# Gated delta-rule attention and feed-forward block: the recurrence written out step by step with fewer transfers, and the rounded feed-forward weights kept on chip

## What is computed

```
q, k, v = silu(conv4(x Wq^T)), silu(conv4(x Wk^T)), silu(conv4(x Wv^T))
beta    = sigmoid(x Wb^T)
# delta rule, chunks of 32 tokens per head, with q and k l2-normed, kb = beta k, vb = beta v
T = inverse(I + strict_lower(kb k^T)) ;  u = T vb ;  w = T kb
step(S): u_adj = u_i - w_i S ;  o_i = q_i S + causal(q_i k_i^T) u_adj ;  S = S + k_i^T u_adj
local_s, local_m, local_l = causal filters of 3, 15 and 63 taps per channel over v
p = softmax((x gate_w + gate_b) / exp(log_temp)), mixed with eps
o = p0 local_s + p1 local_m + p2 local_l + p3 delta + p4 v
x = layernorm(x + rmsnorm(o, norm_w) Wo^T)
h = silu(x W1^T s1) * (x W2^T s2) ;  h = gelu(h H1^T s) ;  h = gelu(h H2^T s)
out = layernorm(x + h W3^T s3)
```

## Time and profile before

| | us |
|---|---|
| median of 3 runs | 2368.65 (2364.51 to 2372.69) |
| the profiled execution, its own time | 2375.07 |
| its span in the profile | 2373.2 |
| project, about 0 to 343 | 343 |
| weights_fir, to about 577 | 234 |
| delta, to about 1036 | 459 |
| ffn, to the end | 1337 |
| TensorE busy (share of the span) | 2094.9 (88%) |
| VectorE / ScalarE / GpSimd busy | 1159.3 / 864.9 / 529.7 |
| bytes moved by DMA | 237.59 MB in 244242 packets |

### The profile page before, as it was taken

How to read it: one execution, slowest core, us unless ns; L and a number is a source line. 1 busy time by engine, 2 the same in 40 slices (tenths; PEclk the granted TensorE clock), 3 DMA queues, 4 the chain that set the end, 5 groups by cost and what they waited for, 6 DMA issues and landing times.

```text
span 2373.2 us, 43639 instructions
## 1 busy us (share of the span) xinstructions
PE 2094.9 (88%) x16936; PEld 1776.2 (75%) x16936; DVE 1159.3 (49%) x1825; ACT 864.9 (36%) x1406; POOL 529.7 (22%) x563
## 2 busy tenths in 40 slices
PE   7888873775888878759999999999999999999998
PEld 5776763675777767648888888888888888888886
DVE  5777768953467657642432343233234324432332
ACT  4545542010333323223443444344334434443442
POOL 1113787864445444410000000000000000000000
PEclk9999996797899988869999999999999999999999
DMA  3775667876778777750000000000000000000000
GB/s 123 199 199 171 200 191 182 284 255 207 201 216 221 210 214 205 209 216 34 19 0 18 18 15 3 18 18 0 18 18 18 0 18 18 10 8 18 18 1 18
DMA packets 244242, 237.59 MB, mean 100 GB/s; under 512 B 145938, under 2 KB 203794, under 8 KB 238354
## 3 DMA queue, kind: packets, MB, share of 16 engines
q1 hardware_dynamic: 227218, 193.74, 28.0%
q10 hardware_dynamic: 16896, 41.95, 5.7%
HBM read 139.96 MB, written 95.68 MB: 99 GB/s over the span
## 4 chain that ended last, share of the span: by engine, by line
PE 53%; issue 1%; DVE 1%; ACT 1%; DMA 0%; POOL 0%; DVEq 0%; SPq 0%; ACTq 0%; POOLq 0%
PE B L1636 48%; PE O L1664 5%; PE T L1592 1%; DVE yb L1763 0%; ACT gate L1702 0%; DMA x<-x_s 0%; DVE stats L1794 0%; ACT L1702 0%; DVE z L1789 0%; DVE xl L1743 0%; DVE z L1785 0%; DVE z L1808 0%; ACT xh L1690 0%; POOL rstd L1844 0%; DVEq L1758 0%
## 5 line engine op out<-in xcount | busy, mean ns | idle before, releaser
L1636 PE MATMUL B<-act1l,wr 128*128 128x512 f32 x1024 | 398.4, 389 | 0.0
L1636 PE MATMUL B<-act0h,wr 128*128 128x512 f32 x1024 | 398.3, 389 | 0.0
L1636 PE MATMUL B<-act0l,wr 128*128 128x512 f32 x1024 | 398.3, 389 | 0.0
L1636 PE MATMUL B<-act1h,wr 128*128 128x512 f32 x1024 | 398.3, 389 | 0.0
L1716 ACT ACTIVATE yb<-B,scol 128x512 f32<-128x512 f32 x256 | 176.2, 688 | 581.0 <-PE B L1636 581.0
L1751 DVE TENSOR_TENSOR act0l<-yb,act0h 128x512 fp32r<-128x512 f32 x256 | 176.1, 688 | 377.8 <-ACT act0h L1719 375.7
L1841 POOL TENSOR_TENSOR rstd<-mv,ln_eps 128x4 f32<-128x4 f32 x16 | 3.2, 199 | 1308.2 <-DVE mv L1802 1308.2
L449 DVE SCALAR_TENSOR_TENSOR acc<-proj,taps,acc 128x512 f32<-128x512 f32 x288 | 214.3, 750 | 86.4 <-ACT acc L395 77.9
L1751 DVE TENSOR_TENSOR act1l<-yb,act1h 128x512 fp32r<-128x512 f32 x128 | 88.6, 692 | 295.5 <-ACT act1h L1719 295.5
L1636 PEld LDWEIGHTS B<-act0h,wr 128*128 128x128 f32 x1024 | 192.2, 188 | 39.9
L1636 PEld LDWEIGHTS B<-act1h,wr 128*128 128x128 f32 x1024 | 192.2, 188 | 39.9
(11 more groups left out here) (171 smaller groups left out, 3234.5 us busy)
## 6 DMA issues: line engine op xcount, KB each, us to landing
qk_s<-yT SPq DMA_DIRECT2D x16, 1024.0 KB, 6.3
kk_s<-kfull SPq DMA_DIRECT2D x16, 1024.0 KB, 6.3
qk<-qk_s SPq DMA_DIRECT2D x32, 512.0 KB, 5.3
wraw<-in_ffn_w ACTq DMA_DIRECT2D x32, 352.0 KB, 6.1
wr_s<-wround ACTq DMA_DIRECT2D x32, 352.0 KB, 4.0
toe<-in_toe_short ACTq DMA_DIRECT2D x32, 320.0 KB, 7.4
xt<-in_xt SPq DMA_DIRECT2D x16, 524.0 KB, 4.3
k_s<-ktok SPq DMA_DIRECT2D x16, 512.0 KB, 7.1
```

Source lines behind the costliest of these rows:

```text
L1636: last = nc.tensor.matmul(B[slot % 4][:, :], w, part, start=(k == 0 and i == 0), stop=(k == kts - 1 and i == len(parts) - 1))
```

## The change

- The recurrence's loops are gone: all 33 steps are written out on every engine, with constants in place of registers. The counter `passed` and its increments go.
- The inverses are stored in another arrangement: `f_s` takes the turned even blocks, `g_s` the even blocks as they are and the odd ones turned, and the odd places of `f_s` are filled with zeros once, by 8 transfers of 256 KB early in `project`. In `delta` one transfer from `f_s` fills the whole left half of `tt` (128 rows) and one from `g_s` the right half; the first round of matmuls reads its operand there, and `first_inv` is gone. A group takes 6 transfers instead of 10.
- `vt` and `mix` become one tile each with 4 places. `slots_in` loads a half group's rows for all 4 sequences, that is for two places, with one transfer each (two each where the places wrap round the end, one step in 4). It stands last in SP's step, behind a wait for `mixed`; the waits for `mixed` and `prep_done` at the front of the step go.
- `xres` has 2 buffers instead of 4, and `wo_raw` lies in `y[1]`.
- The rounded weights are written straight into the tile `wr`, which now lives through `delta` and `ffn`: ScalarE's 32 stores to `wr_s`, the waits for them and for its own rounding, and the 7 loads in `ffn` are gone with their waits.

The diff, cut to its core:

```diff
@@ -245,13 +245,17 @@
+                for first in range(0, GRP, WIN):
+                    for q in range(1, NQ, 2):
+                        sp.dma_start(io["f_s"][first:first + WIN, q, :, :].rearrange("n i j -> n (i j)"),
+                                     zero[:, :, :].rearrange("p h d -> p (h d)")).then_inc(zero_stored, 16)
...
-                        blocks_out("d_s", tri[:, D_OUT[n]:SLOTS:NSUB, :, :], D_OUT[n], inv_stored)
+                        blocks_out("g_s", 0, tri[:, D_OUT[n]:SLOTS:2 * NSUB, :, :], D_OUT[n], inv_stored)
...
-                        blocks_out("t_s", turned_inv[:, :, :, :], T_OUT[n], turned_stored)
+                        blocks_out("g_s", 1, turned_inv[:, 1:NQ:2, :, :], T_OUT[n], turned_stored)
+                        blocks_out("f_s", 0, turned_inv[:, 0:NQ:2, :, :], T_OUT[n], turned_stored)
...
-        def steps(engine, step, first, end):
-
-            loops = (end - first) // RING
-            with engine.Fori(0, loops) as i:
-                for j in range(RING):
-                    step(i * RING + (first + j), (first + j) % RING, i * (RING // 2) + (first + j) // 2)
-            return first + loops * RING
...
-                        sp.dma_start(tt[r][j, :, 0:CH], io["t_s"][mats, 2 * c].rearrange("s i j -> i s j")
-                                     ).then_inc(prep_in[p], 16)
-                        sp.dma_start(tt[r][i, :, CH:HC], io["t_s"][mats, 2 * c + 1].rearrange("s i j -> i s j")
-                                     ).then_inc(prep_in[p], 16)
-                        sp.dma_start(first_inv[p][j, :, :], io["d_s"][mats, 2 * c].rearrange("s i j -> i s j")
-                                     ).then_inc(prep_in[p], 16)
...
+                    for half, name in enumerate(("f_s", "g_s")):
+                        sp.dma_start(tt[r][:, :, half * CH:half * CH + CH], io[name][mats].rearrange("s q i j -> (q i) s j")).then_inc(prep_in[p], 16)
+
+                def slots_in(part, t):
+
+                    rows, u = slice(part * HC, part * HC + HC), 2 * t + part
+                    for first, end in ((0, GB), (GB, BATCH)) if u % RING == RING - 1 else ((0, BATCH),):
+                        r = (u + first // GB) % RING
+                        places = slice(r, r + (end - first) // GB)
...
                     sp.wait_ge(s_ready, u + 1)
-                    sp.sem_inc(passed, 1)
-                    sp.wait_ge(mixed, u)
-                    sp.sem_inc(passed, 1)
-                    sp.wait_ge(prep_done, u + 2)
-                    sp.sem_inc(passed, 1)
-                    if not isinstance(u, int) or u + 3 < GROUPS:
                         group_in(u + 3, (r + 3) % RING, n + 2 if r % 2 else n + 1)
...
-                    if not isinstance(u, int) or u >= 1:
+                    if u >= 1:
                         sp.wait_ge(res_done, u + 1)
                         x_load(u - 1, (r - 1) % RING, n if r % 2 else n - 1)
-                    if not isinstance(u, int) or u >= 3:
+                    if u >= 3:
                         store(u - 3, (r + 1) % RING, n - 1 if r % 2 else n - 2)
+
+                    sp.wait_ge(mixed, u + 1)
+                    t = n + 2 if u % 2 else n + 1
+                    if t < STEPS:
+                        slots_in(1 - u % 2, t)
...
-                            last = nc.tensor.matmul(NA[rows, 0, c, :], lt[r % 2][rows, c, :], first_inv[r % 2][rows, c, :],
+                            last = nc.tensor.matmul(NA[rows, 0, c, :], lt[r % 2][rows, c, :], tt[r][rows, c, CH:HC],
...
-                    act.wait_ge(w_stored[r % 2], n * 16 + 16)
-                    nc.scalar.activation(wround[r % 2][:, :], wraw[r % 2][:, :], ACT.Copy).then_inc(w_rounded, 1)
-                    act.wait_ge(w_rounded, c + 1)
-                    act.dma_start(io["wr_s"][:, bass.ds(c * WCH, WCH)], wround[r % 2][:, :].bitcast(f32)).then_inc(w_stored[r % 2], 16)
+                    nc.scalar.activation(wr[:, c * WCH:c * WCH + WCH], wraw[r % 2][:, :], ACT.Copy).then_inc(w_rounded, 1)
...
-                for u in range(3):
+                for u in range(LAST + 1):
                     step(u, u % RING, u // 2)
-                u = steps(act, step, 3, GROUPS)
...
-                        for n, first, end in WR_PARTS:
-                            sp.dma_start(wr[:, first:end].bitcast(f32), io["wr_s"][:, first:end]).then_inc(wr_in[n], 16)
...
+            late = Stage(nc, sems)
+            with late.ctx:
+
+                keep["wr"] = late.sb("wr", [P, W_END], f32r)
+                delta(nc, sems, io, keep)
+                ffn(nc, sems, io, keep)
```

208 lines of the change are left out of this document (75 added, 133 removed).

## The result

The changed kernel takes 2357.39 us (median of 20 runs, 2329.95 to 2369.49) against 2369.88 for the kernel before (20 runs on the same chips, 2361.76 to 2385.36). By the medians that is 12 us less, 0.5%; the ratio, which is taken over the runs in the faster of the chip's two states alone, is 0.9928, with a 95% interval of 0.9909 to 0.9947. Where 86 us were forecast and 2256 to 2332 was the range, 12 to 17 were found: the direction was right, the size was not.

The account below looks back on a forecast made before the run. `delta` was taken as bound by SP's queue and stops at loop ends, with TensorE's 10.08 us step as floor; -77.8, -2.6, -4, -2 and 0 sum to -86.4 us: 2282 against 2368.65, range 2256 to 2332.

Parts of the forecast that it names:

- The recurrence: `delta`'s 32 steps: from 12.93 to 10.5 us each, -77.8 us in all (-103 to -30).
- the long steps: In `delta` before the change, one step in four takes 19.2 us; laid to the loop's branch and SP's catching up.
- SP's round: SP's transfers for one step of `delta`: from 16 in 12.14 us to 10.5 on average, taken as 9 us.
- The DMA engines' time: Engine time per step of `delta`: 10.0 us before, 9.2 to 10.0 after, against a step of 10.08.
- meetings of the two queues: In `delta`, 0.4 us a step added to the undisturbed 10.08, giving 10.5.
- Rival 1: In `delta`, DMA becomes the bound at a share of 0.84: steps of 12.0 us, 2329 in all; chance 0.18.
- Rival 2: TensorE's straight code in `delta` is fetched too slowly: +259 us, time 2541, deciding from 87 us; chance 0.03.
- the price per piece: In `delta`, 512 more pieces of 128 bytes at 2.03 ns each: 1.04 us a step, against 0.24 by bytes.
- `xl` behind `xh`: Start of `ffn`: without the weight load VectorE's `xl` starts earlier, -4 us (bounds 0 and -4.5).
- `weights_fir` and the start of `delta`: 1 MB less stored in `weights_fir`, -2 us; fewer transfers and clears before `delta`'s first matmuls, -2.6 us.
- project: Eight more transfers and 2 MB in `project`, covered by SP's idle time: 0 us, uncovered +6.
- Rival 3: In `delta`, prefetch distance makes VectorE wait, so each fourth step stays long: time 2339; chance 0.07.

Follow-up runs that it names:

- the two pairs above: Same kernel with `delta`'s tiles on odd multiples of 32 or moved off: all three edits, 2303.81 against 2278.61 us; change with only zero blocks left out, 2344.53 against 2325.91.

## Why the prediction was wrong, step by step

**The step that failed** is in its first paragraph: "the change leaves its matmuls alone, so nothing is to be had there but at its start". It was taken for the whole of `ffn`, and the last line of the prediction names `ffn` other than 1314 us as what would show it wrong. It was 1364. The matmuls were left alone, but not their operand, which went from a multiple of 256 to an odd multiple of 32 (34 us, shown in both directions), nor the place of their code (12.6 us of stops, shown in both directions too: 2344.34 us without them against 2357.39, and 2296.42 with them against 2278.03, the last two in one execution each). Neither was among the costs or the rivals.

**The recurrence, -77.8 forecast, -58.6 found.** What the prediction said of the kernel before held: without branches the long steps stay (19.8 us), without the 16 transfers no fourth step is long, and the residual no longer waits for a transfer. But 10.5 a step was 11.10, for three terms were mis-sized.

- SP's round: "I take 9 [...] so SP stops being behind". Its issues take 10.5 us a step, over the 10.07, since they are held. From 730 until the last group is issued (921) SP never waits for `s_ready`, and the sign named for right, waits of 1 us or more in each step, is missing.
- The DMA engines' time: 9.2 to 10.0 us a step, against 10.7 in the middle steps. The 10.0 that it started from was an average over 410 us with the thin ends in it; over the middle steps the kernel before has 10.4.
- The 0.4 us "for meetings of the two queues", against 1.03.

Rival 1 came true in half: it had DMA bind at 12.0 a step, because a share of 0.84 was the most that this mix can hold. The share held was 0.99 over 100 us of undisturbed steps, and the step was 11.10. Rival 2, with a chance of 0.03, came true in part and was the larger surprise: after 730 TensorE stands for its straight code in most steps, 19.7 us in all and not 87 or more, and the clock, 1.00 up to there, is 0.92 in the mean behind these stops. That the stops go with how hard the queues are pressed is seen in how many are left, in one execution each: nine over 1 us in the change, four without the weight loads, two without the zero pieces, and in the two pairs above 7 and 11 on odd multiples of 32 against 2 and 2. That the crossing of a block of code is hidden, on which the prediction relied, held up to 730 and not behind it. What makes a packet of code late, and whether the first late thing at 730 was code or data, isn't shown. Leaving out the 512 zero pieces, which the prediction had priced at 0.24 or 1.04 us, took 0.91 us off the step, near the price per piece; but the engines' own time fell by 0.6 and SP's issues by 2.0, so it isn't the engines' time that makes that price.

The Trainium skill (DMA: Bandwidth & Descriptors, Specifications), which the prediction held against the change, points the right way with its penalty for small pieces. The runs can't tell a read-modify-write from any other cost per piece.

**The starts.** `xl` behind `xh`: -4 forecast, -4.1 found. `weights_fir` and the start of `delta`: -4.6 forecast; SP starts 2.3 earlier, about what the stores should give, and TensorE 2.8. So the start of `delta` gave 0.5 of the 2.6 there: the first matmul is 8.58 us behind SP's first transfer instead of 9.03. At the first L1176 0.9 is left; where the other 2 went was not followed up. **project**: 0 forecast, and the end of `weights_fir` shows none of the eight more transfers. Rival 3 is out by the absence of long fourth steps.

**The sum.** -86.4 forecast from the profiled execution. Found: -58.6 - 4.1 - 0.9 + 45.2 = -18.4. With the weights and the code where they were and the zero blocks left out, 2278.61 us are measured, near the 2282 of the forecast, but partly for another reason: the last of these edits isn't in the change.

## What to carry to other kernels

When a change allocates, frees or reorders tiles, compare the addresses of all tiles before and after, also in stages that the diff doesn't touch: in this kernel TensorE's two operands want multiples of 256 bytes, the tiles that small transfers land in must not lie on odd multiples of 32 (0 and 128 above a multiple of 256 were good), and a small tile put ahead of them costs about one per cent. Unrolling one loop moves the code of every later one; look for a stop with no semaphore open at its ends and for packets of code inside it, and move it with instructions that aren't executed. Where DMA engines are over 0.9 of their time in use, count pieces before bytes and issues, look at how long single issues are held, and expect straight code to come late.

## What the runs showed of the hardware

- **Place of TensorE's operands.** float32r matmuls of 128x128 by 512 columns at a granted clock of 1.00 stand 226.7 ns apart when weights and streamed tile lie on multiples of 256 (of 1024: the same), 229 with the weights on a multiple of 64 alone, 232 to 234 with either on an odd multiple of 32. For the 256-column ones, 120 ns with both on 256, 113 to 119 otherwise: there the odd places are faster, which I can't explain.
- **Place of what transfers write.** The mix of 128-byte to 4-KB pieces of the recurrence costs 1.99 ns of engine time a packet with its tiles on a multiple of 256 and 2.36 at 224 above, 2.14 at 128 above and 2.27 at 160 above. Places 64 and 192 above weren't tried, and the change, also at 128 above but with the zero pieces, has 2.07, so the smaller of the two steps is hardly clear of the mix; the kernels' times are (2344.53 against 2325.91, 2303.81 against 2278.61). The Trainium skill (DMA: Bandwidth & Descriptors, How a descriptor splits into AXI transactions) has a read start at a multiple of 256 bytes at or below the piece, which would cost extra beats for the one transfer a step that reads these tiles, the store of `y`; the runs don't separate reads of the tiles from writes to them, and the skill's section tells nothing of writes.
- **A loop's stop depends on its place.** About 2 us at each branch back, at 2 of 5 positions tried, and there the whole loop's code comes in again each round (57 to 59 packets of 16 KB in 1100 us, against 3 to 5). The Trainium skill (Runtime: NRT & Kernel Launch, Instruction fetch mechanics) gives blocks of 256 instructions and TensorE a store of 128 KiB, 2048 instructions, which is 8 such blocks, and has a taken branch stall where its target isn't in the current window of two pages. The store fits the positions, the window of two pages doesn't. Without a stop the loop covers 7 blocks (44, 108) or 6 instructions of an eighth (172 + 1626 = 1798); with one it covers 56 or 70 instructions of the eighth. My inference, from five positions, is that fetching ahead then replaces the first block.
- **Late code in straight code.** With the engines at 0.9 to 1.0, TensorE stands up to 3.1 us for its code in the written-out recurrence, nine times over 1 us; at the same load before 730 not once over 1 us, and what decides isn't shown. Five of the nine are followed by a fall of the clock.
- **A held issue.** SP's issue of a transfer of 1024 pieces of 128 bytes takes 1.96 us in the middle right behind another of 1024 pieces, and 0.45 behind 512.
- **Spread.** With the engines full the same code in `delta` took 355 us in one execution and 366 in another (the change, and the one with ffn's code moved); with the zero blocks left out and the tiles on 64 it took 326.1, 326.4, 330.4, 324.2 and 326.5.
